# Taking the upper part of a two-part fp32r split from ACT's write instead of from a mask on DVE

## The reference, cut to what matters

```python
k = int(EXPERT_CAPACITY * t / e)            # 512 tokens of 2048
probs = jax.nn.softmax(scores, axis=-1)
g, m = jax.lax.top_k(probs.transpose(0, 2, 1), k)
xin = x[batch_idx, m]
h = jnp.einsum('nekd,edf->nekf', xin, w1)   # 256 -> 1024
h = jax.nn.gelu(h, approximate=False)
h = jnp.einsum('nekf,efd->nekd', h, w2)     # 1024 -> 256
out = jnp.zeros((n, t, d), dtype=x.dtype).at[batch_idx, m].add(g[..., None] * h)
```

## Time and profile before

| | us |
|---|---|
| median of 3 runs | 1957.0 |
| the three runs | 1957.00, 1952.12, 1957.03 |
| the profiled execution's own time | 1952.26 |
| its span | 1950.5 |

### The profile page before, as it was taken

How to read it: one execution, slowest core, us unless ns; L and a number is a source line. 1 busy time by engine, 2 the same in 40 slices (tenths; PEclk the granted TensorE clock), 3 DMA queues, 4 the chain that set the end, 5 groups by cost and what they waited for, 6 DMA issues and landing times. The chain is left out here.

```text
span 1950.5 us, 34406 instructions
## 1 busy us (share of the span) xinstructions
PE 1722.5 (88%) x12312; PEld 1486.8 (76%) x12312; DVE 1530.8 (78%) x3088; ACT 1351.3 (69%) x2634; POOL 1368.5 (70%) x644
## 2 busy tenths in 40 slices
PE   5778999999999999999999999987662399999997
PEld 4556788887888878888787887876651388888896
DVE  1547888888988889888888888887646788888873
ACT  2368888888888888888889888886421255555562
POOL 0007899898998989989899898999970334444442
PEclk9889999999999999999999999999875599999998
DMA  4003222222222233222332223222211223333331
GB/s 186 1 2 91 63 66 70 70 49 92 67 67 70 51 90 69 67 67 54 88 71 64 64 62 88 64 63 70 67 27 59 76 66 88 85 88 88 86 54 22
DMA packets 110825, 133.11 MB, mean 68 GB/s; under 512 B 8128, under 2 KB 103232, under 8 KB 110400
## 3 DMA queue, kind: packets, MB, share of 16 engines
q1 hardware_dynamic: 98368, 114.13, 21.4%
q0 software_dynamic: 12288, 16.79, 4.9%
HBM read 105.20 MB, written 17.30 MB: 63 GB/s over the span
## 5 line engine op out<-in xcount | busy, mean ns | idle before, releaser
L947 DVE TENSOR_TENSOR_SCAN room<-pD,last,room 128x256 f32<-128x256 f32 x1024 | 691.6, 732 | 79.5 <-PE pD L898 66.6
L966 POOL TENSOR_TENSOR room<-room 128x1024 f32<-128x1024 f32 x256 | 606.4, 2369 | 194.6 <-DVE room L881 156.4
L956 POOL TENSOR_TENSOR room<-room 128x1024 f32<-128x1024 f32 x256 | 606.2, 2368 | 62.5 <-PE pY L915 62.1
L928 ACT ACTIVATE room<-room,fixed,kkT 128x512 f32<-128x512 f32 x512 | 406.3, 806 | 51.6 <-PE pD L898 49.6
L915 PE MATMUL pY<-fixed,room 128*128 128x128 f32 x2048 | 317.9, 279 | 35.3 <-POOL room L956 35.2
L898 PE MATMUL pD<-fixed,room 128*128 128x128 f32 x2048 | 316.7, 278 | 35.0 <-DVE room L947 32.7
L915 PEld LDWEIGHTS pY<-fixed,room 128*128 128x128 f32 x2048 | 246.8, 144 | 88.5 <-POOL room L956 51.7
L898 PEld LDWEIGHTS pD<-fixed,room 128*128 128x128 f32 x2048 | 243.7, 143 | 60.4 <-issue 36.5
L1832 POOL DMA_INDIRECT y_out<-ys,ids x64 | 107.7, 1682 | 214.3 <-DVE ys L1649 122.7
L1769 PE MATMUL po<-w_up,h_up 128*128 128x256 f32 x512 | 146.7, 287 | 4.5 <-DVE ys L1649 4.5
L1769 PE MATMUL po<-w_rest,h_up 128*128 128x256 f32 x512 | 144.9, 283 | 0.0
(11 more groups left out here) (264 smaller groups left out, 3591.3 us busy)
## 6 DMA issues: line engine op xcount, KB each, us to landing
room<-kq_rows SPq DMA_DIRECT2D x256, 256.0 KB, 5.2
w_in<-w_d SPq DMA_DIRECT2D x16, 1024.0 KB
room<-ndS SPq DMA_DIRECT2D x16, 512.0 KB, 3.3
xt<-x_in SPq DMA_DIRECT2D x16, 256.0 KB, 3.0
y_out<-xo SPq DMA_DIRECT2D x16, 256.0 KB, 2.1
xn_rows<-xnC SPq DMA_DIRECT2D x16, 256.0 KB, 2.1
W<-weights SPq DMA_DIRECT2D x1, 3505.5 KB, 13.6
room<-wmod SPq DMA_DIRECT2D x1, 1536.0 KB, 20.6
```

The lines of the kernel that those rows point to most:

```text
L928: act.activation(decT[:, m % 2, t, :], turn2(ndT, it, NT * DI, t * DI, DI), ACT.Identity, bias=ones_s[:, 0:1], scale=turn2(kkT, it, NT * D ...
L947: dve.tensor_tensor_scan(run, pD[h][:, k2 * TB:(k2 + 1) * TB], run, last[:, bass.ds(later(it) * (DS * DT) + m * DT + k, 1)], ALU.mult, ALU ...
L956: pool.tensor_tensor(sq[:, m % 2], st[:, m % 4], kqb[:, m % SLOTS, 1, :].unsqueeze(1).broadcast_to([P, DT, TB]), ALU.mult).then_inc(sem("r ...
L966: pool.tensor_tensor(st[:, m % 4], turn2(u, it, DT * TB).rearrange("p (k t) -> p k t", k=DT), kqb[:, m % SLOTS, 0, :].unsqueeze(1).broadca ...
```

## The change

The mask is left out, and with it the buffer `masked`. ACT now reads the whole value (`w_in`, `hg` or `h1`) and its write into the fp32r buffer rounds it; DVE waits for that write (`upper`) and subtracts what was written from the whole. Each split is one copy on ACT and then one subtraction on DVE. ACT waits for its own earlier writes (`gelu`, `hg`), and the waits for the loaded weights (`w_in`) and for the buffers' last readers (`down_mm`) move from DVE to ACT. The upper part is now rounded, not cut off.

```diff
@@ weights_part (in the looks)
-                    dve.tensor_scalar(to.bitcast(I32), whole.bitcast(I32), UPPER, None, ALU.bitwise_and)\
-                        .then_inc(sem("masked"), 1)
-                    dve.wait_ge(sem("masked"), q + 1)
-                    dve.tensor_tensor(flat(w_rest[:, 0])[:, q * K:(q + 1) * K], whole, to, ALU.subtract)\
-                        .then_inc(sem("w_split"), 1)
+                    at = slice(q * K, (q + 1) * K)
+                    dve.wait_ge(sem("upper"), q + 1)
+                    dve.tensor_tensor(flat(w_rest[:, 0])[:, at], flat(w_in[:, :, :])[:, at],
+                                      flat(w_up[:, 0])[:, at].bitcast(F32), ALU.subtract).then_inc(sem("w_split"), 1)
@@ split (DVE)
-                    dve.tensor_scalar(to.bitcast(I32), whole.bitcast(I32), UPPER, None, ALU.bitwise_and)\
-                        .then_inc(sem("masked"), 1)
-                    dve.wait_ge(sem("masked"), count)
-                    dve.tensor_tensor(rest, whole, to, ALU.subtract).then_inc(sem(done), 1)
+                def split(whole, upper, rest, done, count):
+
+                    dve.wait_ge(sem("upper"), count)
+                    dve.tensor_tensor(rest, whole, upper.bitcast(F32), ALU.subtract).then_inc(sem(done), 1)
@@ put (ACT)
-                    act.wait_ge(sem("masked"), count)
-                    act.activation(to, masked[:, at_ring, :], ACT.Copy).then_inc(sem("upper"), 1)
+                def put(to, whole):
+                    act.activation(to, whole, ACT.Copy).then_inc(sem("upper"), 1)
@@ a_turn (ACT)
-                            if f > 0:
-                                put(h1_up[:, f - 1, :], splits(i, n, ahead) + f, ring(n, f - 1))
-                        put(h1_up[:, FT - 1, :], splits(i, n, ahead) + FT, ring(n, FT - 1))
+                            if f == 0:
+                                act.wait_ge(sem("down_mm"), i * 4 * SL + n * SL)
+                            else:
+                                act.wait_ge(sem("gelu"), i * 4 * FT + n * FT + f)
+                                put(h1_up[:, f - 1, :], h1[:, (f - 1) % 4, :])
+                        act.wait_ge(sem("gelu"), i * 4 * FT + n * FT + FT)
+                        put(h1_up[:, FT - 1, :], h1[:, (FT - 1) % 4, :])
                         if ahead or n < 3:
 
                             modulated((i * 4 + n + 1) * DC, (n + 1) % 2)
                             for c in range(DC):
-                                put(hg_up[:, c, :], splits(i, n, ahead) + FT + c + 1, ring(n, FT + c))
+                                act.wait_ge(sem("hg"), (i * 4 + n + 1) * DC + c + 1)
+                                put(hg_up[:, c, :], hg[:, c, :])
                         if ahead or n < 2:
+                            if n % 2 == 0:
+                                act.wait_ge(sem("w_in"), (i - 1) * 64 + 64 + n // 2 * 32)
+                                act.wait_ge(sem("down_mm"), i * 4 * SL + n * SL)
                             for q in range(WQ // 2):
-                                put_weights(1 - n // 2, n % 2 * (WQ // 2) + q, splits(i, n, ahead) + FT + DC + q + 1,
-                                            ring(n, FT + DC + q))
-
+                                put_weights(1 - n // 2, n % 2 * (WQ // 2) + q)
+
+                act.wait_ge(sem("w_in"), 32)
                 for q in range(WQ):
-                    act.wait_ge(sem("masked"), q + 1)
-                    act.activation(flat(w_up[:, 0])[:, bass.ds(q * K, K)], flat(masked[:, :, :])[:, bass.ds(q * K, K)],
-                                   ACT.Copy).then_inc(sem("upper"), 1)
+                    put_weights(0, q)
```

More of the change, by code:

```diff
@@ L39 @@
 FT = F // P
-UPPER = -4096
 BITS = 30
@@ L1419, in experts @@
         h1 = sb("h1", [P, 4, K])
-        masked = sb("masked", [P, WQ, K])
         h1_up = sb("h1_up", [P, FT, K], F32R)
@@ L1448, in splits @@
             return FIRST + (i - 1) * 4 * PER_LIST + n * PER_LIST - no_weights
-        def ring(n, more):
-            return (FIRST + n * PER_LIST + more) % 4
         def every_turn(eng, a_turn):
@@ L1529, in _ @@
                     last.then_inc(sem("selected"), 1)
-                    if i == LOOKS - WQ:
-                        dve.wait_ge(sem("w_in"), 32)
                     value_part(i)
@@ L1599, in slots_of, with split_weights @@
                         .then_inc(sem("ids"), 1)
[L1601 to L1606, removed]
-                    dve.tensor_scalar(to.bitcast(I32), whole.bitcast(I32), UPPER, None, ALU.bitwise_and)\
-                        .then_inc(sem("masked"), 1)
-                    dve.wait_ge(sem("masked"), count)
-                    dve.tensor_tensor(rest, whole, to, ALU.subtract).then_inc(sem(done), 1)
+                def split(whole, upper, rest, done, count):
+                    dve.wait_ge(sem("upper"), count)
+                    dve.tensor_tensor(rest, whole, upper.bitcast(F32), ALU.subtract).then_inc(sem(done), 1)
                 h = DC * F // 4
-                def split_weights(slot, q, count, at_ring):
-                    n, at = q // 4, (q % 4) * h
-                    split(w_in[:, n, at:at + h], w_rest[:, slot, n, at:at + h], "w_split", count, at_ring)
+                def split_weights(slot, q, count):
+                    n, at = q // 4, slice((q % 4) * h, (q % 4 + 1) * h)
+                    split(w_in[:, n, at], w_up[:, slot, n, at], w_rest[:, slot, n, at], "w_split", count)
                 for m in range(4):
@@ L1622, in _ @@
                 for c in range(DC):
-                    dve.wait_ge(sem("hg"), PER_TURN["hg"] + c + 1)
-                    split(hg[:, c, :], hg_rest[:, c, :], "hg_split", WQ + c + 1, (WQ + c) % 4)
+                    split(hg[:, c, :], hg_up[:, c, :], hg_rest[:, c, :], "hg_split", WQ + c + 1)
                 def a_turn(dve, i, ahead):
@@ L1630, in a_turn @@
                         for f in range(FT):
-                            dve.wait_ge(sem("gelu"), i * 4 * FT + n * FT + f + 1)
                             if f == 0:
                                 dve.wait_ge(sem("down_mm"), i * 4 * SL + n * SL)
-                            split(h1[:, f % 4, :], h1_rest[:, f, :], "h1_split", splits(i, n, ahead) + f + 1,
-                                  ring(n, f))
+                            split(h1[:, f % 4, :], h1_up[:, f, :], h1_rest[:, f, :], "h1_split", splits(i, n, ahead) + f + 1)
                         if not last_list:
                             for c in range(DC):
-                                dve.wait_ge(sem("hg"), (i * 4 + n + 1) * DC + c + 1)
-                                split(hg[:, c, :], hg_rest[:, c, :], "hg_split", splits(i, n, ahead) + FT + c + 1,
-                                      ring(n, FT + c))
+                                split(hg[:, c, :], hg_up[:, c, :], hg_rest[:, c, :], "hg_split",
+                                      splits(i, n, ahead) + FT + c + 1)
                         for c in range(SL):
@@ L1653, in a_turn @@
                             if ahead or n < 2:
-                                if n % 2 == 0 and c == 0:
-                                    dve.wait_ge(sem("w_in"), (i - 1) * 64 + 64 + n // 2 * 32)
                                 for q in ((0, 1), (2,), (3,), ())[c]:
                                     split_weights(1 - n // 2, n % 2 * (WQ // 2) + q,
-                                                  splits(i, n, ahead) + FT + DC + q + 1, ring(n, FT + DC + q))
+                                                  splits(i, n, ahead) + FT + DC + q + 1)
                             if n % 2 == 1 and ahead and c < 2:
@@ L1672, in _, with put_weights @@
                     .then_inc(sem("prob_exp"), 1)
-                def put(to, count, at_ring):
-                    act.wait_ge(sem("masked"), count)
-                    act.activation(to, masked[:, at_ring, :], ACT.Copy).then_inc(sem("upper"), 1)
-                def put_weights(slot, q, count, at_ring):
-                    n, at = q // 4, (q % 4) * K
-                    put(w_up[:, slot, n, at:at + K], count, at_ring)
+                def put(to, whole):
+                    act.activation(to, whole, ACT.Copy).then_inc(sem("upper"), 1)
+                def put_weights(slot, q):
+                    n, at = q // 4, slice((q % 4) * K, (q % 4 + 1) * K)
+                    put(w_up[:, slot, n, at], w_in[:, n, at])
                 def modulated(k_count, b):
```

4 lines of the change are left out of this document (2 added, 2 removed).

## The result

The changed kernel takes 1948.0 us in the median of 17 runs (1943.0 to 1950.4), the kernel before 1954.4 in the median of 17 (1951.4 to 1957.6). The ratio is 0.9966, with a 95% interval of 0.9956 to 0.9975; of 1954.4 us that is 6.6 us less, between 4.9 and 8.6. The forecast was 7.2 us, a ratio of 0.9963.

The account below looks back on a forecast made before the run. PE was taken to bound the lists, DVE's work counting only where PE waits. The terms -5.5 - 2.3 + 0.45 + 0.15 = -7.2 us, taken from a median of 1957.0, gave 1949.8 us; range 1943.4 to 1957.

Parts of the forecast that it names:

- Step 1: The 6 odd lists: PE's waits before output 3 and the second placement product shrink, 0.91 us each, 5.5 us gained.
- the second one: In each odd list, PE's wait for the second `onehot` before its second placement product goes in full, 0.22 us gained.
- At most 1.12 each, all of PE's delay: Upper bound on the gain per odd list, if PE never waits there.
- the term for output 3: In each odd list, `ys` of output 1 comes earlier, so PE starts output 3 0.69 us earlier.
- Step 2: The 8 looks with weights fall from 3.10 to 2.81 us, 2.3 us gained, bounds 1.8 to 2.4.
- Step 3: Start of the first list: PE waits longer for the split of the rows, 0.45 us lost, bounds 0.2 to 0.7.
- Step 4: The last list: the eighth subtraction ends after PE wants it for output 0, 0.15 us lost, bounds 0 to 0.4.
- Step 5: The rest: other masks lie beside a busy PE, and the waits moved to ACT cost nothing; 0 us.
- A: Rival: late ACT copies and handoffs give back the lists' gain, leaving -2.9 us, 1954.1 us; chance 0.21.
- B: Rival: ACT becomes the bound in `ph`, its copies waiting for `gelu`, 20 us slower less 7.2, 1969.8 us; chance 0.05.
- The rule of the Trainium skill that I had weighed: A next Vector instruction waits until DVE's pipe is empty; would give back 0.32 us per odd list, sum -5.3.
- C: Rival: PE never waits in the odd lists, -8.9 us in all, 1948.1 us; chance 0.74 together with the forecast.

Follow-up runs that it names:

- the reordered kernel before: Kernel before, all masks kept, with the second quarter of the next weights split after output 1 instead of after output 0: ratio 0.9998 to before.
- the one with its tuple reordered: Kernel after, with the second quarter of the next weights split after output 1 instead of after output 0: 1943.3 us, ratio 0.9953 to before.

## Why the prediction was right, and where it was not

**What bounds.** Right: PE bounds the lists; 128 masks of 0.45 us put back beside it did not move their period.

**Step 1, the odd lists.** Forecast 0.91 each, measured 48.80 - 47.73 = 1.07 (6.4 us, not 5.5, within the stated 3.0 to 6.7). ACT's chain came out as built: from the last Gelu, `ys` of output 0 starts after 4.74 (forecast 4.77) and `ys` of output 1 after 8.94 (8.99). Output 3 gained 0.73 (0.69). The term that was mis-sized is the second one: between the start of the first placement product and the next `ph` 0.28 was gained (1.10 to 0.82), not 0.22. The remaining 0.06 does not lie in the odd list, which is 1.02 shorter (25.40 to 24.38), but in the even list behind it, where the prediction had nothing (23.40 to 23.36, its hidden chunks 11.16 to 11.18 and now 11.13); I have not traced its cause. "At most 1.12 each, all of PE's delay" was too low too: with almost nothing in PE's way it is 1.24 (48.80 to 47.56). And the reading behind it was wrong: two waits were added up that are one chain. The sum survived since the term for output 3 was made from the times of DVE's chain and the second wait was checked against the end of the second `onehot`; the forecast I made from the waits alone, the reordered kernel before, failed.

**Step 2, the looks.** Right: the looks with weights are 2.81 apart like those without other work, and all looks together 2.4 us shorter (2.3 forecast). The first looks, with pieces of `value`, stay at 2.88.

**Step 3, the first list.** Forecast +0.45; measured from `hg` to `ph` 3.22 before and 3.53 after, +0.31. DVE's part came out as forecast: the second `hg_rest` ends 1.94 after ACT's first copy (1.95 forecast, 1.50 before). What the forecast had wrong is that PE's start behind DVE would stay as it was: it took 0.19 before and takes 0.06 after (1552.15 to 1552.21). Why it is shorter stays open. These are the rows that answer to the earlier trace rows:

```profile
1550.21 1.14 ACT L1651 ACTIVATE hg_up<-hg 128x512 fp32r<-128x512 f32 x2
...
1550.86 1.29 DVE L1594 TENSOR_TENSOR hg_rest<-hg,hg_up 128x512 fp32r<-128x512 f32 x2 [2.67 <-ACT hg_up L1651]
...
1552.21 0.79 PE L1750 MATMUL ph<-hg_up,w_up 128*128 128x512 f32 x1 [2.71 <-DVE hg_rest L1594]
```

**Step 4, the last list.** Forecast +0.15; the outputs took 11.81 us instead of 11.52, +0.29, inside the bounds. The eighth subtraction ends 2.64 after PE's first matmul of output 0, as forecast; PE comes to it 0.19 late in all, and the matmul behind the wait takes 0.39 instead of 0.28, which adds 0.10 that the forecast did not have. With the earlier trace rows goes this row of PEld:

```profile
1924.96 0.19 PEld L1750 LDWEIGHTS po<-w_up,h_up 128*128 128x128 f32 x1 [0.19 <-DVE h_rest L1594]
```

**Step 5.** Right: among ACT's waits only the first load shows, 10.2 us long and before the looks that need it:

```profile
ACT w_up L1651 <- DMA w_in<-w_d: 10.2, 1, 10.2
```

**The sum.** Step by step the traces give -6.4 - 2.3 + 0.3 + 0.3 = -8.1 us. The profiled experts differ by 7.5; the clock in the first list took 0.8 back (below), which no step had. So the forecast of 7.2 stands nearer to the 7.5 than its steps do: the 0.9 that the lists gave beyond it and the clock's 0.8 nearly cancel, and that is luck. The forecast of 1949.8 rested on a median of 1957.0 from three runs, which over 17 is 1954.4; 7.2 below that would be 1947.2, against 1948.0 measured.

**The rivals.** A (late handoffs from ACT) is refuted: DVE follows ACT by 0.03 (`hg_up` ends at 1550.83, `hg_rest` starts at 1550.86), as before. B (ACT as the bound) is refuted, and has more room than I gave it. The rule of the Trainium skill that I had weighed (VectorE: DVE Perf Modes, "The DRAIN you can't avoid") does not hold for these instructions: subtractions are 0.60 apart at a duration of 0.69, and the mask costs 0.34 without and 0.45 with a wait for it. The section itself names an exception, an instruction that is not held; which case applies here no run tells. C, the whole gain, is nearest to what the lists did.

## What to carry to other kernels

When an engine at its limit shows two short waits for the same other engine, ask whether they are one chain before adding them: shorten the chain ahead of the last of them, since relieving the first alone only moves the wait. Work taken off an engine that runs beside the bound counts only where it stands ahead of what the bound waits for; of the 224 masks here, the 3 in that chain in each of 6 lists and the 8 in the looks account for the gain, and taking a single split out of the chain gave the lists' part of the gain with all masks kept.

## What the runs showed of the hardware

**A wait between two DVE instructions costs 0.11 us** where the second needs the first: mask to subtraction 0.45, against 0.34 for a mask nobody waits for.

**PE's clock at the first list varies from execution to execution.** In the looks the granted clock is 0.50, the lower level of 1.2 GHz; PE runs two short matmuls per look there, 0.59 us in 2.81. From the first `ph` on PE works without a gap, and the matmuls' distance falls from 0.43 us to the 0.23 of the later lists (2.4 GHz), after 3.0 us in one execution and after 6.0 in another. The first list's 48 `ph` matmuls took 12.57 to 13.96 us in nine kernels (11.07 to 11.18 in later lists), 13.10 before and 13.91 after. It took 13.91 and 12.74 in two kernels that have the same instructions up to its end, the one after and the one with its tuple reordered; the first 11.18 us of it in these two:

```profile
1552.21:1563.39 11.18, 11.18 (x37) 8.97 (x38) 2.25 (x4) 5.50 (x10) 2.69 (x3) 0.74 0.17 49
```

```profile
1546.01:1557.19 11.18, 11.18 (x42) 9.15 (x43) 2.77 (x4) 6.62 (x12) 2.68 (x3) 0.85 0.18 49
```

The mean granted clock is 0.74 and 0.85 (third from the end). The Trainium skill says of this ramp that it varies between runs of one kernel (TensorE: Matmul & The Clock Gate, Part 1: The HAM clock gate), and the traces agree. It is a spread of 1.4 us that belongs to no change. With matmuls that nobody reads, in PE's gaps before, it was 11.18 in both kernels that had them.

**POOL issues faster without the masks.** An indirect DMA to `y_out` takes POOL 1682 ns on average with them and 1579 after; with 128 idle masks put back in `ph` it was 1575, with 28 beside the outputs 1601, so it is not the number of masks alone. The cause stays open. Only the last four of these issues lie on the path, at the end of the span, and they take 1.55 us each before and after. The group after, from the page:

```profile
L1813 POOL DMA_INDIRECT y_out<-ys,ids x64 | 101.1, 1579 | 213.2 <-DVE ys L1627 128.8
```
